# MLP affine folded into the first weights, VectorE normalises the MLP's tokens, batch norm constants made in the first stage, slots reordered

## What is computed

```
y = (y - mu) / sqrt(var + EPS) * bn_g + bn_b      # batch norm over all images
y = relu(y)
out = feat + y
t = out as tokens x channels
tn = (t - mu) / sqrt(var + EPS) * n3_w + n3_b     # layer norm over channels
h = gelu(tn @ fc1_w.T + fc1_b)
t = t + (h @ fc2_w.T + fc2_b)
```

## Time and profile before

| | us |
|---|---|
| median of 3 runs | 739.96 (736.93 to 745.4) |
| profiled execution | 740.04 |
| its span, first to last instruction | 738.3 |
| PE matmul busy in the span | 628.5 (85%) |
| DVE busy | 468.0 (63%) |
| ACT busy | 345.8 (47%) |
| POOL busy | 249.2 (34%) |
| granted TensorE clock, mean of the span | 0.927 |

### The profile page before, as it was taken

One profiled execution on the slowest core, in us unless ns is written; L12 is line 12 of the kernel. 1 busy time (PEld: TensorE's weight loads), 2 busy tenths in 40 slices (PEclk: granted clock), 3 DMA queues, 4 the chain that ended last, 5 costly groups with the idle time before them and its releaser, 6 DMA issues.

```text
span 738.3 us, 20284 instructions
## 1 busy us (share of the span) xinstructions
PE 628.5 (85%) x8800; PEld 528.7 (72%) x8800; DVE 468.0 (63%) x1032; ACT 345.8 (47%) x548; POOL 249.2 (34%) x260
## 2 busy tenths in 40 slices
PE   5848999999999999574897868898989898988857
PEld 4637787888878788453685646687878787877755
DVE  2577777686777778313364544587768686867445
ACT  4444455463737373106895325544444535361610
POOL 1010203112130303014587427373636454543430
PEclk9868999999999999885798978899999999999997
DMA  7203001010110000001033031221313040400000
GB/s 279 80 1 128 17 3 54 3 54 21 37 40 3 2 3 2 1 29 43 30 72 72 1 72 32 43 57 31 64 25 72 16 73 16 73 16 1 16 16 15
DMA packets 16889, 29.78 MB, mean 40 GB/s; under 512 B 1952, under 2 KB 10400, under 8 KB 15904
## 3 DMA queue, kind: packets, MB, share of 16 engines
q1 hardware_dynamic: 16800, 28.49, 15.4%
HBM read 22.19 MB, written 6.29 MB: 39 GB/s over the span
## 4 chain that ended last, share of the span: by engine, by line
PE 35%; DVE 9%; ACT 5%; POOL 3%; issue 2%; DVEq 0%; POOLq 0%; ACTq 0%
PE ps L201 20%; DVE mx L1391 3%; PE ps L1123 3%; PE ps L1075 3%; PE ps L1101 2%; PE ps L1104 2%; PE ps L986 2%; PE ps L1078 1%; PE ps L1107 1%; DVE acc L1481 1%; DVE st L1333 1%; ACT wide L1211 1%; POOL hl L1297 1%; ACT prob L1240 1%; ACT wide L1201 1%
## 5 line engine op out<-in xcount | busy, mean ns | idle before, releaser
L1311 POOL TENSOR_TENSOR e2l<-prob,e2h 128x1536 f16<-128x1536 f32 x32 | 98.7, 3104 | 16.8 <-ACT e2h L1246 16.8
L201 PE MATMUL ps<-secondh,ch_moe 128*128 128x256 f16 (+1 forms) x320 | 82.5, 265 | 3.4 <-DVE cl_moe L1344 3.1
L508 PE MATMUL ps<-yh,wconvh 128*128 128x256 f16 x288 | 80.4, 279 | 4.2 <-POOL yl L665 4.2
L201 PE MATMUL ps<-secondh,cl_moe 128*128 128x256 f16 (+1 forms) x320 | 82.8, 265 | 0.0
L201 PE MATMUL ps<-secondl,ch_moe 128*128 128x256 f16 (+1 forms) x320 | 82.7, 265 | 0.0
L665 POOL TENSOR_TENSOR yl<-y,yh 128x128 f16<-128x128 f32 x32 | 13.1, 445 | 200.3 <-ACT yh L614 200.3
L508 PE MATMUL ps<-yh,wconvl 128*128 128x256 f16 x288 | 80.5, 279 | 0.0
L508 PE MATMUL ps<-yl,wconvh 128*128 128x256 f16 x288 | 80.2, 278 | 0.0
L1391 DVE TENSOR_REDUCE mx<-ps 128x2 f32<-128x512 f32 (+1 forms) x96 | 65.5, 682 | 22.3 <-PE ps L1078 22.3
L1240 ACT ACTIVATE prob<-ps 128x1536 f32<-128x1536 f32 x32 | 46.4, 1451 | 44.8 <-PE ps L1107 44.8
L1481 DVE SCALAR_TENSOR_TENSOR acc<-ps,gate,acc 128x256 f32<-128x256 f32 x112 | 49.0, 480 | 27.4 <-PE ps L201 27.4
(11 more groups left out here) (221 smaller groups left out, 2086.6 us busy)
## 6 DMA issues: line engine op xcount, KB each, us to landing
weights_stage<-in_second SPq DMA_DIRECT2D x6, 684.0 KB, 4.1
qs<-rope_scratch SPq DMA_DIRECT2D x24, 128.0 KB, 3.7
ks<-rope_scratch SPq DMA_DIRECT2D x24, 128.0 KB, 5.5
weights_stage<-in_wconv SPq DMA_DIRECT2D x6, 384.0 KB, 4.3
xw<-in_xw SPq DMA_DIRECT2D x8, 256.0 KB, 2.8
xc<-in_xc SPq DMA_DIRECT2D x8, 256.0 KB, 2.6
rope_scratch<-rh SPq DMA_DIRECT2D x8, 256.0 KB, 2.3
rope_scratch<-rl SPq DMA_DIRECT2D x8, 256.0 KB, 2.3
```

The lines of the kernel that those rows point to most:

```text
L201: last = nc.tensor.matmul(out_ap, lhs[x], rhs[w], start=done == 0, stop=done == n - 1)
L508: last = nc.tensor.matmul(bank(p, 2 + oh)[:, 0:TOK], w["wconv"][:, c0:c0 + P], im[:, h, dy:dy + HW, dx:dx + HW], start=(tap, h, n) == (0, ...
L1311: nc.gpsimd.tensor_tensor(el[n % 2][:], prob[n % 2][:], eh[n % 2][:], ALU.subtract).then_inc(e2_lo, 1)
```

## The change

- `xc` and `bn` live through both stages. SP loads the first two images of `xc` at the end of stage 1, and DVE and POOL make the batch norm constants there. ACT runs one small GELU at the end of stage 1.
- n3_w is multiplied into the first MLP weights when these are scaled in stage 1 (the chunk of image 2 in three parts, with [P, 1] scales; Identity in place of Copy). n3_b times the raw first weights goes into the bias: SP loads the raw weights at the start of stage 2 into `prob[0]`, PE makes eight matmuls with one column, DVE adds fc1_b into `fc1bias`. PE and DVE do this ahead of their first step.
- `mlp_normalise` is on DVE (one tensor_scalar with two scalars per tile: minus mean, times rstd). POOL leaves out `centre` for the MLP. ACT's `mlp_channels` copies PSUM to `ch`, and `mlp_low` subtracts from PSUM.
- `mlp_base` moves to the slot of `tokens`, ahead of `widen` and `narrow` of earlier images. POOL sets `vh` and `shift` behind `mlp_base(2)`, DVE makes `headb` behind `narrow(0)`.
- In `IMAGE_SLOT`, store and out_project change places, and so do split(0,0) and maxima(-1,0). As one slot is now placed otherwise in `MLP_SLOT`, the merge also puts some steps of the fill in another order.

The diff, cut to its core:

```diff
 MLP_SLOT = [
-    ("load", 0), ("widen", 4), ("mlp_normalise", 2), ("mlp_base", 2), ("mlp_low", 3), ("narrow", 5),
-    ("statistics", 5), ("tokens", 1), ("mlp_channels", 2)]
+    ("load", 0), ("widen", 4), ("mlp_normalise", 2), ("mlp_low", 3), ("narrow", 5), ("statistics", 5),
+    ("tokens", 1), ("mlp_base", 1), ("mlp_channels", 2)]
 IMAGE_SLOT = [
-    ("out_project", 1), ("store", 2), ("moe_statistics", 1), ("split", 0, 0), ("maxima", -1, 0), ("attend", 0,
+    ("store", 2), ("out_project", 1), ("moe_statistics", 1), ("maxima", -1, 0), ("split", 0, 0), ("attend", 0,
...
+        def scaled_parts(c, width):
+            if c == 2:
+                return [(0, HID, small[:, 8:9]), (HID, 2 * HID, small[:, 9:10]), (2 * HID, width, S)]
+            return [(0, width, S)]
...
+            for c in range(2):
+                sp.dma_start(k["xc"][c][:], a["xc"][c * P:(c + 1) * P]).then_inc(first_images, 16)
...
+                    if at == 0:
+                        nc.scalar.activation(small[:, 8:10], col("n3w", 0, 2), ACT.Copy, scale=S).then_inc(n3_set, 1)
...
-                    nc.scalar.activation(high, stage[slot][:, 0:width], ACT.Copy,
-                                         scale=S).then_inc(weights_high, 1)
+                    for c0, c1_, by in scaled_parts(c, width):
+                        last = nc.scalar.activation(high[:, c0:c1_], stage[slot][:, c0:c1_], ACT.Identity, scale=by)
+                    last.then_inc(weights_high, 1)
...
+            nc.scalar.activation(small[:, 32:34], col("bng", 0, 2), ACT.Gelu).then_inc(warm, 1)
...
+            dve.wait_ge(zst_done, 1)
+            for h in range(HALVES):
+                nc.vector.bn_aggr(bn[:, h, 0:2], zst[:, h].rearrange("p b s -> p (b s)")).then_inc(bn_step, 1)
...
+            sp.dma_start(prob[0][:, 0:2 * HID], a["second"][0:P, 0:2 * HID]).then_inc(fc1_raw, 16)
...
             def mlp_channels(c):
-                freed(pe, affine2, c * 2)
+                freed(pe, mlp_lo, c)
...
+            pe.wait_ge(fc1_raw, 16)
+            for m in range(4):
+                for h in range(HALVES):
+                    last = nc.tensor.matmul(bank(1, 1)[:, m:m + 1], prob[0][:, h * HID + m * P:h * HID + (m + 1) * P],
+                                            col("n3b", h), start=h == 0, stop=h == HALVES - 1)
+            last.then_inc(fc1_fold, 1)
...
-                for h in range(HALVES):
-                    nc.scalar.activation(wide[c % 2][:, h, :], bank(0, 1)[:, h * TOK:(h + 1) * TOK], ACT.Identity,
-                                         scale=col("n3w", h), bias=col("n3b", h)).then_inc(affine2, 1)
-                act.wait_ge(affine2, c * 2 + 2)
-                nc.scalar.activation(ch[MLP][c % 2][:], wide[c % 2][:, 0:2, :], ACT.Copy).then_inc(mlp_hi, 1)
+                nc.scalar.activation(flat(ch[MLP][c % 2]), bank(0, 1), ACT.Copy).then_inc(mlp_hi, 1)
...
+                    if m == MLP:
+                        return
                     nc.gpsimd.tensor_tensor(centre[m][:, c, :], mv[m][:, c, :, 0], minus[:], ALU.mult)\
...
+                if c == 2:
+                    for n in range(3):
+                        nc.gpsimd.memset(vh[n][:], 1.0).then_inc(ones_set, 1)
+                    for p in R2:
+                        nc.gpsimd.memset(shift[p][:], 0.0).then_inc(shift_set, 1)
...
+            def mlp_normalise(c):
+                freed(dve, ln["tr"][MLP], c - 1)
+                dve.wait_ge(ln["rstd"][MLP], c + 1)
+                for t in range(TILES):
+                    last = nc.vector.tensor_scalar(tn[MLP][c % 2][:, t, :], t1[c % IN_MLP][:, t, :],
+                                                   mv[MLP][:, c, t, 0:1], rstd[MLP][:, c, t:t + 1], ALU.subtract,
+                                                   ALU.mult)
+                last.then_inc(ln["norm"][MLP], 1)
...
-                nc.vector.tensor_tensor(cl[MLP][c % 2][:], wide[c % 2][:, 0:2, :], ch[MLP][c % 2][:],
+                nc.vector.tensor_tensor(flat(cl[MLP][c % 2]), bank(0, 1), flat(ch[MLP][c % 2]),
                                         ALU.subtract).then_inc(mlp_lo, 1)
...
+                if c == 0:
+                    nc.vector.tensor_copy(headb[:], const("head").unsqueeze(2).to_broadcast([P, L1H, P]))\
+                        .then_inc(head_set, 1)
...
+            dve.wait_ge(fc1_fold, 1)
+            nc.vector.tensor_tensor(fc1bias[:], bank(1, 1)[:, 0:4], col("fc1b", 0, 4), ALU.add).then_inc(fc1_bias, 1)
```

More of the change, by code:

```diff
@@ L89, in build @@
         small = sb(keep, "small", [P, 64])
+        bn = sb(keep, "bn", [P, HALVES, 6])
+        xc = [sb(keep, f"xc{p}", [P, HALVES, TOK]) for p in range(2)]
         hi, lo = {}, {}
@@ L264, in windows @@
         minus_done, centre_done = sems("minus_done"), sems("centre_done")
-        pads_set, half_set = sem("pads_set"), sem("half_set")
+        first_images, n3_set = sem("first_images"), sem("n3_set")
+        pads_set, half_set, bn_step, zst_done, warm = (
+            sem(n) for n in ("pads_set", "half_set", "bn_step", "zst_done", "warm"))
+        bn = k["bn"]
         weights_loaded = sems("weights_loaded")
@@ L626, in weights @@
                     act.wait_ge(weights_loaded[slot], before * 16 + 16)
-                    nc.scalar.activation(high, stage[slot][:, 0:width], ACT.Copy,
-                                         scale=S).then_inc(weights_high, 1)
+                    if c == 2:
+                        act.wait_ge(n3_set, 1)
+                    for c0, c1_, by in scaled_parts(c, width):
+                        last = nc.scalar.activation(high[:, c0:c1_], stage[slot][:, c0:c1_], ACT.Identity, scale=by)
+                    last.then_inc(weights_high, 1)
                     if c >= 2:
-                        nc.scalar.activation(stage[slot][:, 0:width], stage[slot][:, 0:width], ACT.Copy,
-                                             scale=S).then_inc(weights_scaled, 1)
+                        for c0, c1_, by in scaled_parts(c, width):
+                            last = nc.scalar.activation(stage[slot][:, c0:c1_], stage[slot][:, c0:c1_], ACT.Identity,
+                                                        scale=by)
+                        last.then_inc(weights_scaled, 1)
             act.wait_ge(pads_set, 2)
@@ L679, in _ @@
             run({"pool_deviation": deviation, "pool_project": project, "pool_weights": weights})
+            pool.wait_ge(bn_step, 3)
+            nc.gpsimd.tensor_tensor(bn[:, :, 2], bn[:, :, 2], half[:, 0:2], ALU.pow).then_inc(bn_step, 1)
         @block.vector
@@ L839, in conv @@
                 dve.wait_ge(z_done[p], i * 2 + oh + 1)
-                nc.vector.bn_stats(zst[:, oh, c, :], z[:, oh, c * TOK:(c + 1) * TOK])
+                last = nc.vector.bn_stats(zst[:, oh, c, :], z[:, oh, c * TOK:(c + 1) * TOK])
+                if (c, oh) == (B - 1, 1):
+                    last.then_inc(zst_done, 1)
             dve.wait_ge(pads_set, 2)
@@ L878, in one @@
             return sb(own, name, shape, dt)
-        xc, relu = pair("xc", [P, HALVES, TOK]), pair("relu", [P, HALVES, TOK])
+        xc, relu = k["xc"], pair("relu", [P, HALVES, TOK])
         t1, t3 = [one(f"t1{n}", [P, TILES, C]) for n in range(IN_MLP)], one("t3", [P, TILES, C])
@@ L912, in images @@
         half, eps = one("half2", [P, 4]), one("eps2", [P, 4])
-        bn = one("bn", [P, HALVES, 6])
+        bn, fc1bias = k["bn"], one("fc1bias", [P, 4])
         xc_loaded, spilled, stacked, stored = (sems(n) for n in ("xc_loaded", "spilled", "stacked", "stored"))
@@ L943, in images @@
         WEIGHT_BANKS = [((0, 1), 0, 0), ((2, 3), 0, 0), ((0, 1, 2, 3), P, P)]
[L945 removed]
+        rows_zeroed, fc1_raw, fc1_fold, fc1_bias = (sem(n) for n in ("rows_zeroed", "fc1_raw", "fc1_fold", "fc1_bias"))
         block = own.enter_context(nc.Block())
@@ L1211, in widen @@
                     nc.scalar.activation(wide[c % 2][:, m, :], bank(c % 2, 2, 2)[:, m * TOK:(m + 1) * TOK], ACT.Gelu,
-                                         scale=1.0 / S, bias=col("fc1b", m)).then_inc(gelu_done, 1)
+                                         scale=1.0 / S, bias=fc1bias[:, m:m + 1]).then_inc(gelu_done, 1)
                 act.wait_ge(gelu_done, c * 4 + 4)
@@ L1484, in expert @@
                                                    ALU.mult, ALU.add).then_inc(acc_done, 1)
[L1486 to L1496 removed]
+            dve.wait_ge(fc1_fold, 1)
+            nc.vector.tensor_tensor(fc1bias[:], bank(1, 1)[:, 0:4], col("fc1b", 0, 4), ALU.add).then_inc(fc1_bias, 1)
             run({"load": load, "tokens": statistics(MLP, lambda c: t1[c % IN_MLP], t1_done),
[L1498 removed]
+                 "mlp_normalise": mlp_normalise, "mlp_low": mlp_low, "narrow": narrow, "statistics": statistics(QKV, tokens_of, t2_done),
                  "qkv_low": qkv_low,
```

53 lines of the change are left out of this document (22 added, 31 removed), and 2 rows, old and new, of the table ln.

## The result

The changed kernel took 743.03 us (median of 20 executions, 739.37 to 748.27), the kernel before 738.63 us (median of 20, 735.15 to 749.22): 1.0055 times as long, with a 95% interval of 1.003 to 1.008. I had forecast 736.1 us, and the kernel got 4.1 us slower in the median (0.55% of 738.63) and 4.2 us slower in the profiled execution (744.21 against 740.04). That is less than the 1% of my chances, but it lies on the other side of the forecast, just beyond the 743 that I had given for half of the lock-out or a slow DMA; neither of the two happened.

The account below looks back on a forecast made before the run. No engine was full between changeover and about 439 us; queue order bounded that stretch. The walk's 4.5 us gain less 0.6 for reordered slots gave 3.9, so 740.04 became 736.1, range 730 to 743.

Parts of the forecast that it names:

- half of the lock-out or a slow DMA: Upper end of the range, 743: DVE's normalising partly blocked by POOL, or a slow load.
- my walk: Queues followed from stage 2's start through the images to the first maxima at 401.8, 4.5 us earlier.
- then eight matmuls with one column: four like them took 0.61 in stage 1, so eight about 1.1: Bias fold on PE at stage 2's start, after the raw weights land: about 1.1 us.
- memory 3.2: POOL's setting of memory (2.6 and 0.6), now ahead of hl(0): 3.2 us.
- the third rival: Every DVE normalise locked out by POOL: 745.8, or 749 with the first rival's 3.3 on top; chance 0.06.
- narrow 0.7, headb 1.7: DVE's steps after narrow(0), ahead of statistics and normalise(4): 0.7 us, then the headb cast 1.7.
- Sum 0.6 against: Reordered slots in the fill: two statistics steps cost 1.0 and 0.8, narrow(7) gives 1.2 back.
- The credit of 1.2: In the fill, narrow(7) ahead of maxima(0,10) covers PE's wait for DVE's maximum: 1.2 us back.
- the start and the moved fillers eat the rest: Changeover and after: slow landing, slower normalise, stage 1's cost and omitted waits leave 0.6 us, 739.4; chance 0.23.
- the closing hole: Full PE clock through widen(0), widen(6) and maxima, fillers finding gaps: 3 to 6 us more, 731; chance 0.24.
- the signs that I listed: First relu near 331.9, transposes near 337.4, tensor_scalar near 0.37, rot at 386, maxima(0,0) at 401.8, among others.
- my three signs of being wrong: First transposes before 335.9, hl(0) not waiting for the memory, or normalise over 1 us.

Follow-up runs that it names:

- all_three: The changed kernel with the bias fold moved late, memsets and headb cast back at stage 2's front, and maxima ahead of statistics; 729.28 us, ratio 0.9865.
- maxima_first: The changed kernel with maxima(0,1) and maxima(0,5) again ahead of statistics(5) and statistics(6) in the fill; 740.7 us, ratio 1.002.
- constants_only: The kernel before with only the batch norm constants, first two image loads and GELU table moved into stage 1; 737.57 us, ratio 0.9975.
- pe_kept_busy: all_three plus matmuls nobody reads, 24 ahead of the first transposes and 12 ahead of each of mlp_channels(0) and mlp_channels(1); 729.72 us, ratio 0.9883.

## Why the prediction was wrong, step by step

Each mark of my walk, counted from 327.97, beside the same mark of the trace after, counted from 329.66:

| step | forecast | measured | error added here |
|---|---|---|---|
| first relu | 3.9 | 3.7 | -0.2 |
| PE starts the fold | 7.3 | 7.3 | +0.2 |
| first transposes | 9.4 | 11.7 | **+2.3** |
| normalise(2) ends | 23.7 | 26.0 | 0 |
| hl(0) ends | 30.3 | 31.4 | -1.2 |
| narrow(0) ends | 33.0 | 34.3 | +0.2 |
| normalise(4) ends | 39.7 | 42.9 | **+1.9** |
| rot starts | 58.0 | 61.4 | +0.2 |
| maxima(0,0) on PE | 73.8 | 77.9 | +0.7 |
| first exp | 109.0 | 115.1 | **+2.0** |

The errors sum to 6.1 us. The mark itself came 1.7 later in this execution, and 0.3 were lost behind the first exp (297.7 against 297.4): 736.1 + 6.1 + 1.7 + 0.3 = 744.2, and the profiled execution took 744.21. Image 2 of stage 1, for which I had put "nothing", is 1.0 longer in this trace (35.42 against 34.46) and 0.7 in the mean of the changed kernels; the rest of the 1.7 is less than the scatter of the start of image 2 between traces (83 to 88 us). Two smaller errors of the walk: the terms of its last line give 385.5 and not 386.0, and the way from the low half's end to the first maxima took 10.6 (396.91 to 407.56) instead of 9.9, with PE ready 2.34 before the data.

**The start: wrong in one term, the largest of the three errors that decided it.** The early constants (2.2, forecast 2.4 to 2.6) and the transfer (3.67, forecast 3.5) were right. The step that failed is "then eight matmuls with one column: four like them took 0.61 in stage 1, so eight about 1.1"; they took 3.58. The row says x4, and I read four matmuls. But the trace after records x16 for the eight matmuls of L1198: a matmul of f32 operands counts as two. So the x4 was two matmuls. The 16 matmuls of L368 stand in the trace of before as 32, from 16.8 to 20.3, 0.22 us for each of the 16 at full clock, which makes eight 1.8 us. The summary of the eight of them that read `wf` (ns, least, median and most):

```profile
L368 PEld LDWEIGHTS ps<-vec,wf x16: 186/192/192, 16.8 to 19.8; 128*128 128x128 f32 x16
L368 PE MATMUL ps<-vec,wf x16: 250/250/271, 16.8 to 19.8; 128*128 128x1 f32 x16
```

In the same way the engine's state was left out: L368 ran at a granted clock of 1.00, the fold ran behind a pause of PE of 8.3 us, and the table of after gives 0.50 for 333 to 341 us, the lower of the two levels. That doubles it again, to 3.58. The weight loads fill 3.49 of these 3.58. TensorE: Matmul & The Clock Gate of the Trainium skill (section Weight-path perf modes — Fast Weight Load (FWL) and DoubleRow) says that the fast weight load isn't used for FP32 weights. The traces agree: at the full clock a load of 128x128 f32 took 0.19 (L368, before), one of f16 0.10 (L203, after).

**The walk to normalise(2): right.** Three images forward of the first transposes it took 14.2, forecast 14.3. The memsets were overestimated: I took "memory 3.2" from 2.61 and its smaller companion, and the 2.61 had run beside headb; alone the two took 1.53 and 0.56. That gave 1.2 back.

**headb: the third rival's mechanism, at another instruction.** The step that failed is "narrow 0.7, headb 1.7", where the cast took 3.18: a duration of 1.69 taken from one place and carried to a place with another neighbour. I had asked of the eight normalisations whether POOL works beside them, found that it doesn't, and was right (0.401 to 0.414 in all 16; the pair 0.74, forecast 0.75). Of headb, which I had moved myself behind narrow(0), just where POOL runs hl, I didn't ask. The cast's 1.23 alone and its end 1.1 behind hl's end fit a cast that stood until POOL was done. The Trainium skill, SBUF — State Buffer, section SBUF: two separate sides, has this lock for VectorE's two-port modes as well as for its operations with two SBUF inputs; by that rule the cast is exposed too, and the trace agrees: 3.18 beside hl against 1.23. That the cast runs in such a mode is my inference; what is shown is that its time depends on POOL. Undone alone, it gives 0.44%.

**The order swaps: right in sign, too small.** The step that failed is "Sum 0.6 against"; the trace after has 2.7. The term that was mis-sized is the price of the two steps, 1.0 and 0.8: from maxima(0,0) to maxima(0,9), the part that holds both, the trace after has 25.4 (407.56 to 432.99) and before 21.6 (406.38 to 428.02), 3.8 more instead of 1.8. The credit of 1.2 came: from maxima(0,9) to the first exp 11.7 against 12.8. Of the 3.8, 2.24 are PE's two waits, each longer by 1.12. The rest goes with the clock: right behind the first wait the matmuls at 413.90 take 0.42 where those at 408 take 0.27, and the granted clock over this part is 0.82, before 0.88. The clock's share scatters. The four other changed kernels with the statistics ahead have 23.6 to 23.7 in this part (0.89 to 0.90 granted), all_three and the three kernels built on it 21.2 to 21.5 (0.92), and maxima_first 19.8 (1.00). So 2.1 to 2.5 us for the swaps is what repeats, and what the clock adds to it in one execution is not settled; the median gives 0.35% for undoing them.

**No-ops: right.** The swaps of store with out_project and split with maxima changed nothing in the last stage (297.7 against 297.4), and the table load at 350.71 became one in stage 1 at 329.21 that nobody waited for.

**The rivals.** The one I had at 739.4 ("the start and the moved fillers eat the rest") was the nearest, and fell short, because it varied the sizes that I had put down as unsure (the transfer, normalise) and not the one I took for known. The time of the closing hole (731) is reached once the three placements are mended, 729.28, but by these repairs and only in part by the rival's mechanism: in all_three widen(0), from 345.22, still begins at the half clock (0.42 each to 347.1), and from the first maxima to the first exp 0.89 was granted. Of the signs that I listed, relu (counted from the mark) and tensor_scalar came out as forecast and rot and maxima(0,0) did not. The first transposes, 2.3 behind their forecast from the mark, pointed to the faulty step at once. None of my three signs of being wrong appeared: two of them looked for steps that come too early, the third for a long normalise, and none for a long fold or a long cast.

## What to carry to other kernels

Before a row's duration is moved to another place, ask three things of it: how many instructions of the program its count stands for, at which granted clock it ran, and which engine worked beside it. Small preparatory work belongs in a gap behind the first steps that feed everybody, not ahead of them: the fold was 3.4 to 3.6 us of PE in either place, and cost 2.5 at the front and nothing seen in PE's gaps, and its transfer 3.7 more. When a change loses little, undo its parts one by one: here a change that measured 0.55% slower held a version 1.35% faster than the kernel before.

## What the runs showed of the hardware that I had not expected

- A matmul with f32 operands appears as two records of matmul and two of weight load, while the four f32 transposes of tokens stand as four. With one column it cost 0.22 us at the full and 0.45 at the half clock (3.58 by eight).
- One DVE cast of 128x2048 from f32 to bf16, both in SBUF, took 1.23, 1.69, 2.18 or 3.18 us. What POOL ran beside it goes with the steps from 1.23 to 1.69 and to 3.18; the 2.18 (constants_only) had the same memsets beside it, begun at the same distance, and what made it longer than 1.69 is open. The lengths repeat: 1.69 or 1.70 in six of the twelve traces, 3.18 or 3.19 in the four that have it behind narrow(0). It works both ways: POOL's three memsets took 2.61 beside the cast of 1.69 and 1.53 without it, one of the three 1.63 instead of 0.55.
- From 340 to 350 in pe_kept_busy PE was busy for 9.94 of the 10 us and was granted 0.54.
- The time of an unchanged kernel followed the clock granted over the whole span: of the 29 executions of the kernel before beside the first four runs, the shortest two (734.36, 734.76) were granted 0.936 and 0.939, the longest two (746.69, 745.83) 0.918 and 0.924. The profiled executions of constants_only and of maxima_first, both granted 0.934 over the span, lie 4 us under their own medians (733.33 to 737.57, 736.65 to 740.7). So causes of 0.5% were readable only from a mark inside the trace.
